# A post-norm decoder layer on one core: cross-attention transpositions placed ahead of the weighted sum, residual additions on GpSimd

## The reference

```python
x = _layernorm(x + _L0_attn_ref(x, ...))             # recurrent attention, 16 heads
x = _layernorm(x + _L0_xattn_ref(x, ctx_512, ctx_512))
x = _layernorm(x + _L0_ffn_ref(x, ...))              # gated FFN, 1408 wide
# _L0_xattn_ref: 32 query heads, 8 key heads, 16 channels a head, 512 keys
scores = jnp.einsum('bkgsd,bktd->bkgst', qh, kh) * scale
attn = jax.nn.softmax(scores, axis=-1)
out = jnp.einsum('bkgst,bktd->bkgsd', attn, vh)
```

## Time and profile before

| | |
|---|---|
| time before, median of 3 runs | 2198.46 us (2197.83 to 2201.05) |
| the profiled execution's own time | 2199.38 us |
| its span | 2197.7 us |
| TensorE busy | 2087.7 us (95%) |
| VectorE busy | 1539.1 us (70%) |
| ScalarE busy | 974.7 us (44%) |
| GpSimd busy | 548.3 us (25%) |
| steady part of the cross-attention looked at below | 1383 to 1718 us of the span |

### The profile page before, as it was taken

One profiled execution on the slowest core, in us unless ns is written; L12 is line 12 of the kernel. 1 busy time (PEld: TensorE's weight loads), 2 busy tenths in 40 slices (PEclk: granted clock), 3 DMA queues, 4 the chain that ended last, 5 costly groups with the idle time before them and its releaser, 6 DMA issues. The chain is left out here.

```text
span 2197.7 us, 32758 instructions
## 1 busy us (share of the span) xinstructions
PE 2087.7 (95%) x11316; PEld 1545.1 (70%) x11316; DVE 1539.1 (70%) x2451; ACT 974.7 (44%) x2236; POOL 548.3 (25%) x630
## 2 busy tenths in 40 slices
PE   7999999999999999999999977999999979999996
PEld 6787887887878887888888764434333357877774
DVE  4776776766767766767667775999999555555557
ACT  3444443443443434444444331788888832121110
POOL 3132241251251242242242113212222011111111
PEclk9999999999999999999999986999999999999998
DMA  4000100100100100100000000111110010000002
GB/s 153 1 1 10 35 1 11 34 1 11 34 10 1 34 10 1 34 10 17 19 10 1 1 1 15 24 24 29 25 29 18 7 30 29 14 29 23 20 14 77
DMA packets 58440, 46.55 MB, mean 21 GB/s; under 512 B 14416, under 2 KB 47184, under 8 KB 58320
## 3 DMA queue, kind: packets, MB, share of 16 engines
q1 hardware_dynamic: 58320, 44.85, 6.8%
HBM read 32.78 MB, written 4.19 MB: 17 GB/s over the span
## 5 line engine op out<-in xcount | busy, mean ns | idle before, releaser
L1275 DVE TENSOR_REDUCE x_nm<-x_ps 128x1 f32<-128x512 f32 x512 | 322.0, 683 | 27.7 <-PE x_ps L1084 25.6
L1252 ACT ACTIVATE x_prob<-x_ps 128x512 f32<-128x512 f32 x512 | 278.6, 604 | 62.9 <-PE x_ps L1106 62.4
L356 POOL TENSOR_TENSOR a_causal<-a_causal,a_mask 128x128 f32<-128x128 f32 x128 | 68.5, 545 | 594.2 <-ACT a_causal L618 592.7
L64 PE MATMUL a_ps<-a_vg_hi,a_xT_lo 128*128 128x512 f32 x512 | 209.2, 409 | 1.0 <-DVE a_vg_lo L810 1.0
L65 PE MATMUL a_ps<-a_vg_lo,a_xT_hi 128*128 128x512 f32 x512 | 200.2, 391 | 0.0
L66 PE MATMUL a_ps<-a_vg_hi,a_xT_hi 128*128 128x512 f32 x512 | 200.2, 391 | 0.0
L1084 PE MATMUL x_ps<-x_ks,x_qs 64*128 64x512 f32 x512 | 196.6, 478 | 2.7 <-DVE x_nm L1275 2.4
L1106 PE MATMUL x_ps<-x_qs,x_ks 64*128 64x512 f32 x512 | 185.1, 451 | 4.5 <-ACT x_prob L1252 4.4
L469 PE MATMUL a_ps<-a_right_hi,a_left 128*128 128x256 f32 (+2 forms) x512 | 166.4, 341 | 21.7 <-issue 16.5
L1084 PEld LDWEIGHTS x_ps<-x_ks,x_qs 64*128 64x128 f32 x512 | 84.0, 194 | 133.5 <-DVE x_nm L1275 83.8
L596 ACT CAST a_right_hi<-a_og 64x512 fp32r<-64x512 f32 x128 | 79.3, 619 | 194.4 <-DVE a_og L784 192.0
(11 more groups left out here) (159 smaller groups left out, 4597.0 us busy)
## 6 DMA issues: line engine op xcount, KB each, us to landing
a_raw_vg<-in_L_attn_Wv_dram SPq DMA_DIRECT2D x8, 512.0 KB, 4.1
a_raw_vg<-in_L_attn_Wg_dram SPq DMA_DIRECT2D x8, 512.0 KB, 6.3
a_raw_qks<-in_L_attn_Wo_dram SPq DMA_DIRECT2D x8, 512.0 KB, 3.6
out_dram<-acc SPq DMA_DIRECT2D x8, 512.0 KB, 3.3
x_ks<-x_ks SPq DMA_DIRECT2D x30, 128.0 KB, 2.3
x_xrows<-acc SPq DMA_DIRECT2D x13, 256.0 KB, 2.8
acc<-in_x_dram SPq DMA_DIRECT2D x3, 1024.0 KB, 9.8
f_raw_down<-in_L_ffn_down_w_dram SPq DMA_DIRECT2D x11, 256.0 KB, 2.9
```

The lines of the kernel that those rows point to most:

```text
L64: pe.matmul(out, w_lo, x_hi, start=start, stop=False)
L1252: nc.scalar.activation(prob[:, s % 4, par, :], score_bank(q, s, par), ACT.Exp, scale=X_SCALE).then_inc(exp_done[par], 1)
L1275: nc.vector.tensor_reduce(nm[:, q % 2, i % 4, par, i // 4:i // 4 + 1], max_bank(u, q, i, par), AX.X, ALU.max, negate=True).then_inc(max_re ...
```

## The change

Four things change, all in `phase_cross`.

1. `one_transpose` puts the eight blocks of transpositions of a unit into the odd steps, between the four score matmuls and the weighted sum. A pair of steps becomes: four matmuls, four matmuls, transpositions, weighted sum. ScalarE's copies follow into the odd steps.
2. VectorE's `normalise` moves with them: to step 7 for half 1 of the unit before (was 3) and to step 15 for half 0 (was 13), in both cases ahead of the two reductions of its step. Before, it stood behind them.
3. `add` runs on GpSimd, at the head of its work of the next unit, and VectorE's product waits until `avn` was added (two additions back).
4. The statistics of the layer norm move from steps 6 to 12 to steps 9 to 15, the aggregation to step 0 of the next unit.

```diff
+            def add(u, b, q, g):
+                pool.wait_ge(avn_ready, 2 * u + g + 1)
+                a = acc[:, bass.ds(b * TT, TT), P * q + 64 * g:P * q + 64 * (g + 1)]
+                nc.gpsimd.tensor_tensor(a, a, avn[:, g].rearrange("p t h c -> p t (h c)"), ALU.add).then_inc(added, 1)
...
                     u = b * 4 + q
+                    if not (first and q == 0):
+                        for g in range(2):
+                            add(u - 1, b if q else b - 1, (q - 1) % 4, g)
                     if not (last and q == 3):
                         split_max(u + 1, (q + 1) % 4)
...
-                if s == 0 and not (first and q == 0) and not (last and q == 3):
-                    pe.wait_ge(opsT_ready, TILES * (u + 1) + 4)
+                if s == 1 and not start and not end:
+                    pe.wait_ge(avn_ready, 2 * u - 1)
                     transpose_operands(u + 1, (q + 1) % 4, 4)
...
+                if s == 7 and not start:
+                    if more:
+                        pe.wait_ge(opsT_ready, TILES * (u + 2) + 2)
...
+                    transpose_weighted(u - 1, 1)
...
+                if s == 15:
+                    if more:
+                        pe.wait_ge(opsT_ready, TILES * (u + 2) + 4)
...
                     transpose_weighted(u, 0)
...
                 nc.vector.reciprocal(rec[:, g, :, :], rows[:, :, :, DH]).then_inc(rec_ready, 1)
                 dve.wait_ge(rec_ready, 2 * u + g + 1)
+                wait(dve, added, 2 * u + g - 1)
...
+                        if s == 7 and not (first and q == 0):
+                            normalise(u - 1, 1)
+                        if s == 15:
+                            normalise(u, 0)
...
                                 reduce_max(u + ahead, (q + ahead) % 4, i)
-                        if s == 3 and not (first and q == 0):
-                            normalise(u - 1, 1)
-                        if s == 4 and not (first and q == 0):
-                            add(u - 1, b if q else b - 1, (q - 1) % 4, 1)
...
-                        if s == 13:
-                            normalise(u, 0)
-                        if s == 14:
-                            add(u, b, q, 0)
```

More of the change, by code:

```diff
@@ L1055, in _ @@
             each_batch(pool, body)
+            for g in range(2):
+                add(UNITS - 1, B - 1, 3, g)
         @block.tensor
@@ L1151, in one_transpose @@
                 more = not (last and q > 1)
-                if s == 0 and not (first and q == 0) and not (last and q == 3):
-                    pe.wait_ge(opsT_ready, TILES * (u + 1) + 4)
+                start, end = first and q == 0, last and q == 3
+                if s == 1 and not start and not end:
+                    pe.wait_ge(avn_ready, 2 * u - 1)
                     transpose_operands(u + 1, (q + 1) % 4, 4)
-                if s == 2 and not (first and q == 0):
-                    if last and q == 3:
+                if s == 3 and more:
+                    pe.wait_ge(opsT_ready, TILES * (u + 2))
+                    if start:
+                        pe.wait_ge(mT_ready, 1)
+                    transpose_operands(u + 2, (q + 2) % 4, 0)
+                if s == 5 and more:
+                    pe.wait_ge(opsT_ready, TILES * (u + 2) + 1)
+                    transpose_operands(u + 2, (q + 2) % 4, 1)
+                if s == 7 and not start:
+                    if more:
+                        pe.wait_ge(opsT_ready, TILES * (u + 2) + 2)
+                    elif not end:
+                        pe.wait_ge(opsT_ready, TILES * (u + 2))
+                    else:
                         pe.wait_ge(avn_ready, 2 * u - 1)
-                    else:
[L1159 to L1169, removed]
+                    transpose_weighted(u - 1, 1)
+                if s == 9 and more:
+                    if start:
+                        pe.wait_ge(opsT_ready, TILES * (u + 2) + 2)
+                    else:
+                        pe.wait_ge(avn_ready, 2 * u)
+                    transpose_operands(u + 2, (q + 2) % 4, 2)
+                if s == 11 and not end:
                     if more:
@@ L1172, in one_transpose @@
                     else:
-                        wait(pe, avn_ready, 2 * u)
+                        pe.wait_ge(avn_ready, 2 * u)
                     transpose_max(u + 1, (q + 1) % 4)
-                if s == 12:
-                    if last and q == 3:
+                if s == 13 and more:
+                    pe.wait_ge(mT_ready, u + 2)
+                    transpose_operands(u + 2, (q + 2) % 4, 3)
+                if s == 15:
+                    if more:
+                        pe.wait_ge(opsT_ready, TILES * (u + 2) + 4)
+                    elif not end:
+                        pe.wait_ge(mT_ready, u + 2)
+                    else:
                         pe.wait_ge(avn_ready, 2 * u)
-                    else:
-                        pe.wait_ge(mT_ready, u + 2)
                     transpose_weighted(u, 0)
-                if s == 14 and more:
-                    pe.wait_ge(avn_ready, 2 * u + 1)
-                    transpose_operands(u + 2, (q + 2) % 4, 3)
             def body(b, first, last):
@@ L1253, in body @@
                                                  scale=X_SCALE).then_inc(exp_done[par], 1)
-                        if s == 0 and not (first and q == 0) and not (last and q == 3):
+                        if s == 1 and not (first and q == 0) and not (last and q == 3):
                             copy_queries(u + 1, (q + 1) % 4, 4)
-                        if s == 4 and more:
+                        if s == 3 and more:
                             copy_keys(u + 2, (q + 2) % 4)
-                        if s in (6, 8) and more:
-                            copy_queries(u + 2, (q + 2) % 4, s // 2 - 2)
-                        if s == 10 and not (last and q == 3):
+                        if s in (5, 9, 13) and more:
+                            copy_queries(u + 2, (q + 2) % 4, (s - 1) // 4)
+                        if s == 11 and not (last and q == 3):
                             copy_max(u + 1, (q + 1) % 4)
-                        if s == 14 and more:
-                            copy_queries(u + 2, (q + 2) % 4, 3)
             each_batch(act, body)
@@ L1285, in normalise @@
                                         ALU.mult).then_inc(avn_ready, 1)
[L1287 to L1291, removed]
             rows = acc[:, 0:TT, 0:P].rearrange("p t (h c) -> p t h c", c=DH)
@@ L1313, in body @@
                         norm_of = (B - 1, B - 1, B - 1) if first else (b - 1, 0, B + b - 1)
-                        if stats_unit and s == 6 and not first:
+                        if s == 7 and not (first and q == 0):
+                            normalise(u - 1, 1)
+                        if s == 15:
+                            normalise(u, 0)
+                        if stats_unit and s == 9 and not first:
                             dve.wait_ge(added, 2 * u)
-                        if stats_unit and s == 14:
+                        if use_unit and s == 0:
                             dve.wait_ge(norm.stats_ready, norm_of[2] + 1)
@@ L1320, in body @@
                                 reduce_max(u + ahead, (q + ahead) % 4, i)
-                        if s == 3 and not (first and q == 0):
-                            normalise(u - 1, 1)
-                        if s == 4 and not (first and q == 0):
-                            add(u - 1, b if q else b - 1, (q - 1) % 4, 1)
-                        if stats_unit and s in (6, 8, 10, 12):
-                            norm.statistics(*norm_of[:2], tiles=[s // 2 - 3])
-                        if stats_unit and s == 14:
+                        if stats_unit and s in (9, 11, 13, 15):
+                            norm.statistics(*norm_of[:2], tiles=[(s - 9) // 2])
+                        if use_unit and s == 0:
                             norm.aggregate(norm_of[1])
@@ L1330, in body @@
                             norm.apply(dve, *norm_of, tiles=[s // 2 - 3])
-                        if s == 13:
-                            normalise(u, 0)
-                        if s == 14:
-                            add(u, b, q, 0)
             each_batch(dve, body)
             normalise(UNITS - 1, 1)
-            add(UNITS - 1, B - 1, 3, 1)
 def phase_ffn(nc, gate_w, up_w, down_w, gate_s, up_s, down_s, out, acc, ident, norm):
```

## The result

The changed kernel takes 2245.6 us (median of 4 runs, 2244.0 to 2247.6) against 2198.3 before (4 runs): a ratio of 1.0213, 95% interval 1.0195 to 1.0231. That is 47 us slower; 2240 was predicted, with a range of 2209 to 2262. The span of the profiled execution grew by 46.1 us, from 2197.7 to 2243.8.

The account below looks back on a forecast made before the run. TensorE was taken to pace the pairs, with a three-bank round trip of 1.28 us. 110 pairs at 3.29 plus 27 x 0.42 made 373.2 against 335; with 0.6, 2.4 and 0.35 added, 2240 us, range 2209 to 2262.

Parts of the forecast that it names:

- The trip through three banks, 1.28, sets the fourth turn: In a cross-attention pair, the fourth matmul waits 1.28 us for its bank, where back to back it would come at 0.99.
- The transpositions are paid in full behind the second group: Moved there, their 0.59 no longer fills the wait: a pair takes 3.29 us instead of 2.90, 0.39 more.
- The normalisation's 0.42: On VectorE, normalising ahead of its step's reductions delays the next pair by 0.42 us, 27 times in the stretch, 11.3 us.
- The additions cost nothing either way: Moving them to GpSimd frees 11.1 us of VectorE work, counted as no gain; a GpSimd addition of 0.76 delays nothing.
- The norm's work fits into the room of 0.8: Statistics and application on VectorE, 0.6 us each in eight pairs of 32, fit its spare 0.8 a pair at no cost.
- its 373.2: Forecast for the cross-attention's 110 pairs: 361.9 us plus 11.3 for normalisations, against 335 before.
- Head and tail: Cross-attention's ends: +0.6 for one block at half clock (twice 0.59, less 0.59 saved), +2.4 in units 14 and 15, +0.35 last addition.
- that VectorE sets the pace of the ordinary pair: Rival: VectorE paces the cross-attention and the change relieves it, total about 2184 us; chance 0.1.
- That changes between kinds of matmul are what costs: Rival: on TensorE a pair has one such change less, 3.11 us, total 2220 or 2209; chance 0.2 within the forecast.
- the two groups now standing together saved something: On TensorE, one drain less a pair, bounded by 0.09 us; by that rule alone the total would be 2230.

Follow-up runs that it names:

- e6: Changed kernel with exponentials of only 256 of the 512 columns: 2239.2 us, one run.
- e8: Changed kernel with both exponentials and maxima taken over only 256 of the 512 columns: 2200.1 us, one run.
- e1: Changed kernel with every block of transpositions put back between the two groups of four score matmuls: 2194.9 us, 0.9986 of before.
- e9: Changed kernel with one transposition instead of four in the four query blocks of a unit, exponents scaled down: 2232.7 us, one run.
- e10: Kernel before the change with one transposition instead of four in the four query blocks of a unit, exponents scaled down: 2196.4 us, one run.
- e3: Changed kernel with the normalisation put behind the two reductions of its step: 2233.4 us, 1.0171 of before.
- e4: Kernel before the change with only the additions moved to GpSimd: 2198.3 us, ratio 1.0001.
- e5: Changed kernel with the additions back on VectorE, behind the reductions of the next step: 2250.2 us, 1.0246 of before.
- e11: e1 with the layer norm's work spread over more steps, none next to a normalisation: 2188.2 us, 0.9950 of before.
- e7: Changed kernel with maxima reduced over only 256 of the 512 columns: 2221.2 us, one run.
- e2: e1 with only two of a block's four transpositions between the groups and two behind: 2222.5 us, 1.0122 of before.

## Why the prediction was right

*The trip through three banks, 1.28, sets the fourth turn.* Right to the hundredth (the difference of the first two rows that I cited for it is 1.27, that of the other two 1.28): 1.28 in after, and e6 to e8 show that it is the trip, both trips, and not the sum of TensorE's work.

*The transpositions are paid in full behind the second group.* Right: 0.43 + 0.58 + 1.00 behind the fourth turn, 3.29 a pair as predicted. e1 gives the 0.39 back, e9 shows the 0.33 of left-out work in full where e10 shows 0.17 to 0.20 of it.

*The normalisation's 0.42.* Measured 0.40 (3.69 against 3.29), and 11.2 us in e3 for 27 in the stretch. In eight of them the product also waits for the addition on GpSimd that the change brought, 0.12 instead of 0.03 behind the reciprocal, and the pair takes 0.09 more, 0.7 us. The prediction had named this wait and given it no cost.

*The additions cost nothing either way.* In the kernel before yes (e4), in after not quite: 4.6 us by the medians (e5). GpSimd's addition took 0.73, the straight line had given 0.76; apart from these eight products nobody waited for it.

*The norm's work fits into the room of 0.8.* This step failed, and it is about half of the 6.0 us by which the stretch exceeded its 373.2. The room is one pair's, and here three things meet in one. At step 15 of a unit with statistics, the normalisation holds back two reductions, a statistics instruction follows, then the aggregation:

```profile
1509.96 0.26 DVE L1301 RECIPROCAL x_rec<-x_ps 128x16 f32<-128x16 f32 x1 [0.60 <-PE x_ps L1137]
1510.34 0.42 DVE L1304 TENSOR_TENSOR x_avn<-x_ps,x_rec 128x256 f32<-128x256 f32 x1
1510.68 1.28 DVE L1295 TENSOR_REDUCE x_nm<-x_ps 128x1 f32<-128x512 f32 x2
1511.88 0.68 DVE L97 BATCH_NORM_STATS2 norm_stats<-acc 128x6 f32 x1
1512.68 1.29 DVE L1295 TENSOR_REDUCE x_nm<-x_ps 128x1 f32<-128x512 f32 x2
```

and TensorE's fourth turn of the maxima waits for it:

```profile
1513.43 0.50 PE L1095 MATMUL x_ps<-x_ks,x_qs 64*128 64x512 f32 x1 [0.68 <-DVE x_nm L1295]
```

Four such pairs took 4.41 to 4.59 instead of 3.69 or 3.78, 3.1 us. The prediction had named this work as hidden in the room; the sum should have added at least 0.6 for the statistics where they follow a normalisation.

*Terms that the sum lacked.* In the loop's eight units the pair in which ScalarE copies `avs` ahead of its exponentials takes 3.36 or 3.39 instead of 3.29 or 3.24: 0.07 + 0.15, 1.8 us in all. In e6, with exponentials of half the columns, these pairs are 3.28 and 3.24, so the time comes from ScalarE; why only in the loop stays open. One fall of TensorE's clock, below, took some 1.2 us. The other pairs of the loop are 0.01 to 0.02 longer, some 0.5, and the three pairs where the rotation of banks starts over (see e11) took 0.4 more. The blocks of the maxima are 0.05 shorter, -0.7.

*Head and tail.* +0.9 in the head against 2 x 0.59, and the first pair of the stretch took 2.70, 0.6 less than the sum's 3.29, as predicted; +2.3 in the tail against +2.75.

So the 5.6 us between 2240 and 2245.6 are not one error but the rest of several of both signs. That the total came so near is in part luck; that the ordinary pair came out at 3.29 is not.

The rivals: that VectorE sets the pace of the ordinary pair is refuted by e4 for the kernel before and, with 27% less of its work and pairs of 3.29, by e7 for after. That changes between kinds of matmul are what costs: the price exists and is larger than I had it (0.15 a block, e2), but the change has as many blocks as the kernel before, so it moved nothing here. That the two groups now standing together saved something doesn't show: the pair came out at 3.29 with no such saving in its sum, and a block takes 0.59 with scores behind it (before) and 0.58 with the weighted sum behind it (after).

## What to carry to other kernels

With n buffers in turn (three here), n+1 uses in a row are held by the trip of one buffer, producer, consumer and both signals, where this trip (1.28 here) is longer than the producer needs for n uses (0.99). Work of the producer's that doesn't need these buffers (a filler) is free between the uses as far as it fits into this wait, and costs its full length behind them. So count the uses between two fillers against the buffers before moving a filler, and look in the trace for a spot where the filler is missing. Busy shares of 97% and 94% told nothing of this; a stretch of the same code without the filler told it to a hundredth.

## What the runs showed of the hardware that I had not expected

A block of 128-column transpositions between other matmuls costs 0.26 us for one (e9), 0.37 for two (e2) and 0.58 for four (after): about 0.15 for the block and 0.11 for each. Two half blocks are dearer than a whole one.

TensorE's clock fell once inside the stretch, right behind the pile-up shown above, in which it had stood idle for 0.68 us:

```profile
1510.00:1514.00 4.00, 3.21 (x17) 1.11 (x11) 3.75 (x9) 2.34 (x5) 0.00 (x0) 1.00 0.02 4
1514.00:1516.00 2.00, 2.00 (x12) 0.47 (x11) 1.43 (x6) 0.58 (x1) 1.59 (x3) 0.60 0.00 0
1516.00:1518.00 2.00, 2.00 (x12) 1.01 (x8) 0.87 (x2) 1.42 (x3) 0.33 (x1) 0.55 0.00 0
1518.00:1520.00 2.00, 2.00 (x16) 0.75 (x15) 1.62 (x3) 1.71 (x4) 0.00 (x0) 1.00 0.00 0
```

The granted clock went from 1.00 (2.4 GHz) to about 0.5 (1.2 GHz) for some 3.5 us; the weighted sum in it took 1.86 instead of 1.00. The other three pile-ups of after, with 0.59 to 0.69 of idle time at the same place, had no such fall, and an idle time of 0.95 in before (ahead of 1573.97) had none either. In e9 it was the first pile-up that had one, behind 0.60 of idle time (0.59 and 0.56 in the 4 us from 1433), and the 1.79 in e5 was followed by 6.8 us at 0.50. So the idle time alone doesn't decide it.
